# Four graph layers in one kernel: a base table for the sort, two accumulators for layer 0's sums, one last stage

## What is computed

```python
x = x + L0(h)   # attention: softmax over the edges of a source node, weighted rows summed at dst
x = x + L1(h)   # rows of dst, times a filter, summed at src; residual layers on the nodes
x = x + L2(h)   # a normed message per edge, summed at dst; gated update
x = x + L3(h)   # messages as below
# L3: agg = segment_sum(W * (h[dst] @ lin1.T), src);  return h + ssp(agg @ lin2.T + lin2_b)
# ssp(v) = softplus(v) - log(2)
# L0: out = segment_sum(msg, col);  out = where(deg > 0, out, xh)
```

## Time and profile before

| | |
|---|---|
| median of 3 runs | 7450.98 us |
| profiled execution | 7452.6 us, its span 7451.0 us |
| busy: TensorE / VectorE / GpSimd / ScalarE | 65% / 63% / 60% / 35% |
| sort: first to last send | 332.4 to 1584.9 us |
| layer 0's sums: first to last load issue of GpSimd | 2940.2 to 3433.1 us |
| last three stages | 7375.0 to 7451.0 us |

### The profile page before, as it was taken

The page is one execution under the profiler, slowest core; times in us unless marked ns, Lnnn a source line. Parts: engine busy times, 40 slices in busy tenths (PEclk is TensorE's granted clock), DMA queues, the critical chain, the costliest instruction groups (busy, mean ns, idle before and its releaser), DMA issues. The chain is left out here.

```text
span 7451.0 us, 136629 instructions
## 1 busy us (share of the span) xinstructions
PE 4824.4 (65%) x26170; PEld 3695.7 (50%) x26171; DVE 4677.1 (63%) x15439; ACT 2640.5 (35%) x6893; POOL 4448.7 (60%) x5261
## 2 busy tenths in 40 slices
PE   6777777730555554773566666666667664998896
PEld 4555555520444443662355555334555554666664
DVE  8666665634444443666555555777777775777776
ACT  2244444410222222664400000563333334444443
POOL 0165666652777777662277777207777771777774
PEclk9978787765555555666566667788888886778777
DMA  1144444460222222441133333103333321333332
GB/s 59 51 119 118 120 119 119 117 71 20 58 58 58 58 57 71 113 112 48 43 78 78 78 78 78 25 15 78 74 74 74 75 68 31 73 72 72 72 72 52
DMA packets 858580, 541.08 MB, mean 73 GB/s; under 512 B 652181, under 2 KB 757481, under 8 KB 858089
## 3 DMA queue, kind: packets, MB, share of 16 engines
q0 software_dynamic: 148032, 300.00, 14.9%
q1 hardware_dynamic: 608520, 192.51, 12.5%
q10 hardware_dynamic: 101920, 47.37, 2.6%
HBM read 411.68 MB, written 127.68 MB: 72 GB/s over the span
## 5 line engine op out<-in xcount | busy, mean ns | idle before, releaser
L1339 POOL DMA_INDIRECT l2e_rows<-l_rows,l2e_idx x832 | 847.2, 1018 | 566.9 <-DVE l2e_idx L1347 328.4
L798 POOL DMA_INDIRECT src_records<-sort_rec,sort_idx x784 | 768.5, 980 | 552.4 <-DVEq L676 319.4
L1339 POOL DMA_INDIRECT l1e_rows<-l_rows,l1e_idx x832 | 796.8, 958 | 490.0 <-DVE l1e_idx L1347 296.3
L1339 POOL DMA_INDIRECT l3e_rows<-l_rows,l3e_idx x832 | 804.1, 967 | 424.8 <-DVE l3e_idx L1347 221.4
L1222 POOL DMA_INDIRECT dst_rows<-l0d_out,l0d_idx x832 | 812.3, 976 | 276.5 <-issue 196.7
L2115 PE MATMUL l2e_pV<-l2e_rows,ident 128*128 128x512 f32 x416 | 302.3, 817 | 355.6 <-DMA l2e_rows<-l_rows,l2e_idx 355.1
L1194 PE MATMUL l0d_pX<-table,l0d_ohT 128*128 x1664 | 461.2, 457 | 86.3 <-issue 69.3
L1321 PE MATMUL l0m_pR<-l0m_rows,l0m_oh 128*128 128x129 f32 x1664 | 352.8, 378 | 200.2 <-DVE h_nodes L1292 140.9
L1685 PE MATMUL l1e_pG<-k_weights,l1e_dT 64*128 64x128 f32 x1664 | 220.5, 403 | 374.7 <-DVE l1e_prod L1714 371.7
L1194 PEld LDWEIGHTS l0d_pX<-table,l0d_ohT 128*128 128x128 f32 x1664 | 393.1, 326 | 139.8 <-issue 139.7
L1186 PE MATMUL l0d_pT<-identb,l0d_oh 128*128 128x128 bf16 x832 | 125.4, 305 | 472.8 <-DVE l0d_oh L1167 472.8
(11 more groups left out here) (406 smaller groups left out, 13955.7 us busy)
## 6 DMA issues: line engine op xcount, KB each, us to landing
sort_rows<-lo_rows SPq DMA_DIRECT2D x196, 256.0 KB
sort_rec<-rec ACTq DMA_DIRECT2D x98, 472.0 KB
l0m_rows<-dst_rows SPq DMA_DIRECT2D x416, 66.0 KB, 2.0
l0m_rows<-dst_rows POOLq DMA_DIRECT2D x416, 66.0 KB
l1e_rec<-src_records SPq DMA_DIRECT2D x832, 32.0 KB
l2e_lrow<-dst_local SPq DMA_DIRECT2D x208, 128.0 KB
l3e_rec<-src_records SPq DMA_DIRECT2D x832, 25.0 KB
l0d_meta<-src_records SPq DMA_DIRECT2D x832, 6.0 KB
```

The lines of the kernel that those rows point to most:

```text
L798: e.indirect_dma_start(kn.by_src_rec[:, :], bass.IndirectOffsetOnAxis(ap=r["idx"][:, st.quad, j:j + 1], axis=0), r["rec"][:, st.quad, j, : ...
L1339: e.indirect_dma_start(r["rows"][:, st.quad, j, 0:width], None, table[:, :], bass.IndirectOffsetOnAxis(ap=r["idx"][:, st.quad, j:j + 1], a ...
```

## The change

**The sort's base table.** The front's count of destinations keeps its tiles apart: step i's matmul multiplies with a matrix that has ones in column i only, so row i of `hd` gets the counts of step i. `offsets` makes from it, for each step (partition) and tile, the base of every block, as two numbers whose sum it is (`tile_base`, half and remainder, in 16 bits). In the sort, `drank` is then three matmuls: the one-hots of the step times "before", and row i of each part of the table, picked by one column of the identity (and of twice the identity) that is read 128 times. The copy `carry`, the row `dbase`, and the waits for them are gone.

**Record loads.** `load_records` moves from ScalarE to SyncE, one round later than the rows of keys; SyncE first waits for the clearing of the record buffers.

**Layer 0's sums.** Tiles 0 and 2 of a step add to `sums0`, tiles 1 and 3 to a second accumulator `odd`; an add waits for the last one of its own accumulator. `l0_table` clears `odd` too, and `l0_close` adds it to `sums0` with one instruction of 128 x 6321.

**The end of layer 3.** `l3_finish` replaces the three stages: per group of 7 blocks the product, clamp, exp, ln, the maximum, seven turns, and two additions; SyncE stores a group when its additions are done. PSUM holds two groups of products (four before), and nothing clears `AC`.

```diff
                                     row(kn, "b_att")[:, 0:2 * HEADS], ALU.add).then_inc(r["s_ok"], 1)
             e.wait_ge(r["pe"], n)
-            ch(e.tensor_reduce(kn.tot_dst[:, :], r["hd"][:, 0:GT * NB].rearrange("p (t b) -> p b t", b=NB), AX, ALU.add))
+            ch(e.tensor_copy(kn.tile_counts[:, :], r["hd"][:, 0:GT * NB]))
...
-                    e.matmul(r["hd"][:, 0:GT * NB], kn.onesh[:, :], r["hi"][:, i % 2, 0, :, :].rearrange("p t b -> p (t b)"),
+                    e.matmul(r["hd"][:, 0:GT * NB], r["to_row"][:, P - i:2 * P - i], r["hi"][:, i % 2, 0, :, :].rearrange("p t b -> p (t b)"),
...
+                     skip_group_check=True)
+            e.wait_ge(r["grouped"], 1)
+            e.matmul(r["small"][:, 2 * NB:3 * NB], kn.before[:, :], r["group"][:, :], start=True, stop=True,
+                     skip_group_check=True)
+            e.matmul(r["small"][:, 3 * NB:4 * NB], kn.ones[:, :], r["group"][:, :], start=True, stop=True,
                      skip_group_check=True).then_inc(r["sums"], 1)
...
+            counts = kn.tile_counts[:, :].rearrange("p (t b) -> p t b", b=NB)
+            e.tensor_reduce(r["group"][:, :], counts.rearrange("p t b -> p b t"), AX, ALU.add).then_inc(r["grouped"], 1)
...
+            ch(e.tensor_tensor(r["row"][:, 0, :], r["small"][:, 2 * NB:3 * NB], r["excl"][:, 0:NB], ALU.add))
+            for t in range(GT - 1):
+                ch.wait()
+                ch(e.tensor_tensor(r["row"][:, t + 1, :], r["row"][:, t, :], counts[:, t, :], ALU.add))
+            ch.wait()
+            rows = r["row"][:, :, :].rearrange("p t b -> p (t b)")
+            ch(e.tensor_scalar(kn.tile_base[:, 0, :], rows, 0.5, None, ALU.mult))
+            ch.wait()
+            ch(e.scalar_tensor_tensor(kn.tile_base[:, 1, :], kn.tile_base[:, 0, :], -2.0, rows, ALU.mult, ALU.add))
             e.wait_ge(r["counted"], 2)
...
+            def load_records(st):
+                wait_quad_free(e, r, "sent", st, GT)
+                e.dma_start(r["rec"][:, st.quad, :, 0:NREC], rec_tiles[:, bass.ds(st.i * GT, GT), :]
+                            ).then_inc(r[f"rec_ld{st.quad}"], 16)
+
             e.wait_ge(kn.low_st, 32)
-            run_steps(e, ch, [(load_rows, 0)], n)
+            e.wait_ge(r["cleared"], 1)
+            run_steps(e, ch, [(load_rows, 0), (load_records, 1)], n, 4)
...
-                e.wait_ge(r["carried"], st.i + 2)
...
-            run_steps(e, ch, [(load_records, 0), (wide_hot, 1), (low, 0), (keys, 2), (mask, 1), (carry, 2)], n, 4)
+            run_steps(e, ch, [(wide_hot, 1), (low, 0), (keys, 2), (mask, 1)], n, 4)
...
             def drank(st):
-                e.wait_ge(r["carried"], st.i + 1)
+                wait_step(e, r["hot"], st)
                 wait_step(e, r["dtaken"], st, 1)
-                e.matmul(r["drank"][:, 0:(GT + 1) * NB].rearrange("p (t b) -> p t b", b=NB), r["onerow"][0:1, :],
-                         r["dbase"][0:1, None, :].to_broadcast([1, GT + 1, NB]), start=True, stop=False,
-                         skip_group_check=True)
-                e.matmul(r["drank"][:, 0:GT * NB], kn.beforeh[:, :],
-                         r["ohhi"][:, st.quad, 0, :, :].rearrange("p t b -> p (t b)"), start=False, stop=False,
-                         skip_group_check=True)
-                for j in range(GT):
-                    ins = e.matmul(r["drank"][:, (j + 1) * NB:(GT + 1) * NB].rearrange("p (t b) -> p t b", b=NB),
-                                   kn.onesh[:, :], r["ohhi"][:, st.quad, 0, j:j + 1, :].to_broadcast([P, GT - j, NB]),
-                                   start=False, stop=(j == GT - 1), skip_group_check=True)
+                out = r["drank"][:, 0:GT * NB]
+                e.matmul(out, kn.beforeh[:, :], r["ohhi"][:, st.quad, 0, :, :].rearrange("p t b -> p (t b)"),
+                         start=True, stop=False, skip_group_check=True)
+                for k, t in enumerate((kn.twiceh, kn.identh)):
+                    ins = e.matmul(out, t[:, bass.ds(st.i, 1)].to_broadcast([P, P]), kn.tile_base[:, k, :],
+                                   start=False, stop=(k == 1), skip_group_check=True)
                 ins.then_inc(r["dranked"], 1)
...
             ch(e.memset(kn.sums0[:, :], 0.0))
+            ch(e.memset(kn.odd[:, :], 0.0))
             e.wait_ge(r["got"], 16 * NB)
...
-                wait_step(e, r["added"], st, 1)
                 for j in range(G):
-                    if j:
+                    if j == 1:
+                        wait_step(e, r["added"], st, 1)
+                    elif j:
+                        ch.until(at[j % 2])
+                    else:
                         ch.wait()
-                    acc = kn.sums0[:, bass.ds(blocks[j] * AW, AW)]
+                    acc = (kn.odd if j % 2 else kn.sums0)[:, bass.ds(blocks[j] * AW, AW)]
                     ins = e.tensor_tensor(acc, acc, sums(r, st, j), ALU.add)
                     if j < G - 1:
                         ch(ins)
+                        at[j % 2] = ch.done
...
             sums = kn.sums0[:, :].rearrange("p (b w) -> p b w", w=AW)
+            ch(e.tensor_tensor(kn.sums0[:, :], kn.sums0[:, :], kn.odd[:, :], ALU.add))
+            ch.wait()
...
+def l3_finish(kn):
+
+    whole = N // P
+
     def build(r):
+        def tensor(e, ch):
+            def product(k):
+                if k > 1:
+                    e.wait_ge(r["maxed"], k - 1)
+                src = wide(kn, kn.AC, k)
+                for h in range(2):
+                    ins = e.matmul(r["p"][:, k % 2, h, 0:SEC], mat(kn, "lin2"), src[:, h, :], start=True, stop=True)
+                ins.then_inc(r["product"], 1)
+
+            def turn(k):
+                e.wait_ge(r["maxed"], k + 1)
+                for q in halves(k):
+                    if q > 1:
+                        e.wait_ge(r["added"], q - 1)
+                    for j, b in enumerate(members(q)):
+                        ins = e.transpose(four(r["pA"], q)[:, j, :], kn.MT[:, b, :], kn.ident[:, :])
+                    ins.then_inc(r["turned"], 1)
+            product(0)
+            product(1)
+            for k in range(GROUPS):
+                if k + 2 < GROUPS:
+                    product(k + 2)
+                turn(k)
+
+        def vector(e, ch):
+            ch(e.tensor_scalar(r["less"][:, :], vec(kn, "lin2_b"), 1.0, -LN2, ALU.mult, ALU.add))
+
+            def clamp(k):
+                e.wait_ge(r["product"], k + 1)
+                if k > 1:
+                    e.wait_ge(r["maxed"], k - 1)
+                e.tensor_scalar(r["part"][:, k % 2, :, :], r["p"][:, k % 2, :, 0:SEC], vec(kn, "lin2_b"), CAP, ALU.add, ALU.min
+                                ).then_inc(r["clamped"], 1)
+
+            def keep(k):
+                x = group(kn.X, k)
+                e.tensor_tensor(x, x, group(kn.Hn, k), ALU.add).then_inc(r["kept"], 1)
+
+            def smooth(k):
+                e.wait_ge(r["logged"], k + 1)
+                e.scalar_tensor_tensor(wide(kn, kn.MT, k), r["p"][:, k % 2, :, 0:SEC], r["less"][:, 0:1],
+                                       r["part"][:, k % 2, :, :], ALU.add, ALU.max).then_inc(r["maxed"], 1)
+
+            def add(k):
+                e.wait_ge(r["kept"], k + 1)
+                for q in halves(k):
+                    e.wait_ge(r["turned"], q + 1)
+                    x = few_blocks(kn.X, q)
+                    e.tensor_tensor(x, x, four(r["pA"], q), ALU.add).then_inc(r["added"], 1)
+            clamp(0)
+            clamp(1)
+            ch.wait()
+            for k in range(GROUPS + 1):
+                if k < GROUPS:
+                    keep(k)
+                    smooth(k)
+                if k + 2 < GROUPS:
+                    clamp(k + 2)
+                if k:
+                    add(k - 1)
+
+        def scalar(e, ch):
+            e.preload_act_table_set("natural_log_exp_and_others")
+            for k in range(GROUPS + 1):
+                if k < GROUPS:
+                    e.wait_ge(r["clamped"], k + 1)
+                    ch(e.activation(r["part"][:, k % 2, :, :], r["part"][:, k % 2, :, :], ACT.Exp))
+                if k < GROUPS:
+                    ch.wait()
+                    e.activation(r["part"][:, k % 2, :, :], r["part"][:, k % 2, :, :], ACT.Ln, bias=kn.half1[:, 0:1], scale=0.5
+                                 ).then_inc(r["logged"], 1)
+
         def sync(e, ch):
-            full = (N // P) * P
-            e.dma_start(kn.out[0:full, :].rearrange("(b p) h -> p b h", p=P), kn.X[:, 0:N // P, :]).then_inc(r["st"], 16)
-            e.dma_start(kn.out[full:N, :], kn.X[0:N - full, N // P, :]).then_inc(r["st"], 16)
-            e.wait_ge(r["st"], 32)
-        return dict(sync=sync)
-    phase(kn, "store", build, sems=["st"])
+            out = kn.out[0:whole * P, :].rearrange("(b p) h -> p b h", p=P)
+            for k in range(GROUPS):
+                e.wait_ge(r["added"], 2 * k + 2)
+                last = min(GROUPS * (k + 1), whole)
```

(11 more changed lines are left out.)

66 lines of the change are left out of this document (18 added, 48 removed).

## The result

The changed kernel takes 7200.98 us (median of three runs, 7198.4 to 7212.5) against 7450.98: a ratio of 0.967, 95% interval 0.966 to 0.969. The profiled execution took 7198.4 us with a span of 7196.8, so the span fell by 254.2 us where 266.7 were forecast.

The account below looks back on a forecast made before the run. No engine bounds the whole; in the sort a ring of waits sets the pace. Sends -250.6, set-up +4, sums -3, merge +6.9, last stage -24 give -266.7: 7451.0 to 7184 us, range for 8 in 10 7163 to 7265.

Parts of the forecast that it names:

- the ring: Sort: waits linking GpSimd's sends, ScalarE's wait for them, its base-row copy and VectorE; 25.38 us for two steps.
- the new bound: Sort after the change: GpSimd's sends bound it at 10.22 us per step, -250.6 us; chance 0.66.
- The first rival: Sort: VectorE and TensorE, handing work to each other, hold a step at about 11 us, 7261 us; chance 0.20.
- the low clock: Sort: the clock falls to TensorE's low level, 13 us per step, 7458 us at worst; chance 0.03.
- the issue time alone: Sort: moving the loads and dropping the copy saves only their issue time, 7378 us; chance 0.05.
- the slower SyncE order: Sort: SyncE's queue delays key rows behind sends, closing in three steps; 7553 us at a 25 us load; chance 0.02.
- One sign: Sort: ScalarE's wait for landed sends would be gone and its idle time would lie with VectorE's compares.
- The ring is cut at both joints.: Sort: no wait for sends stands ahead of ScalarE's work, and VectorE needs no copy; part of the -250.6 us.
- the price per send, 1.278 us: Sort: GpSimd's time per send, issue gaps included, from the trace of before; 784 sends take 1001.9 us.
- the first row of the ledger: Sort: change of the sends' stretch, first to last; forecast -250.6 us, measured -228.8.
- `drank` on TensorE: Sort: three matmuls of the remaining shape cost at most 1.05 us per step, where `drank` took 2.21.
- Set-up: Before the sort: table operations about 1 us, SyncE's wait for clearing the records 3 us; +4 us, bounds 1 and 8.

Follow-up runs that it names:

- the second run: Kernel before with only the base table, record loads left on ScalarE: 8973.0 us (ratio 0.999); on another chip 7415.5 us (0.994).

## Why the prediction was right, and where it was off

The forecast was 7184 us with 7163 to 7265; measured 7201. Leaving the untouched stages aside, its terms came to -242.3 us instead of -266.7. The 11.9 us from those stages brought the measured time nearer to the forecast, and that is luck: without them it would be 7213.

**The ring and the new bound.** Right: the ring ran through ScalarE's wait for sends, and GpSimd's own sends are what is left. The first rival (11 us a step), the low clock, the issue time alone (57 us, where the loads alone gave 225) and the slower SyncE order did not come about; the granted clock in the sort rose from 0.80 to 0.88, and SyncE's order cost nothing: VectorE's 1.9 us per round at the key rows, seen in the waits, stand beside GpSimd's sends. One sign came out otherwise: ScalarE's idle time lies mostly before the landing of the record load (299.6 us) and less before VectorE's compares (121.6).

**"The ring is cut at both joints."** Half true. It rests on one cut: the loads alone give the 225 us, the table alone 42, and the table on top of the loads nothing in the sort (1019.8 against 1023.7 us). The forecast of the sum did not depend on it, but whoever had made only the table, on the argument that VectorE then needs no copy, would have been wrong by 170 us or more; I made that mistake in the expectation of the second run.

**The mis-sized term: the price per send, 1.278 us.** It measured 1.306, and 784 times 0.028 are the 22 us by which the first row of the ledger falls short. Some 17 of them are longer sends, 1.001 us instead of 0.980. I took the price from a trace in which GpSimd was idle for 5 us in every second step; there, fewer sends met VectorE's compares. With GpSimd busy all the time, each round's compares meet one: 0.045 us over the shortest send on average, 0.024 before. The other 5 us are a slip in the working: it spread the gaps named "issue", which stood before 695 of the 747 sends, over all 747, 0.298 us each, while the gap of the others was counted with GpSimd's waits; with GpSimd busy all the time it is 0.305 us before every send. The run with the compare twice shows the tie.

**`drank` on TensorE.** Two matmuls with the read-128-times column and one with ordinary weights take 63.1 us in 92 steps, 0.69 us a step (at most 1.05 forecast); the column costs nothing extra: 0.33 us for each of the three matmuls, 0.1 for each weight load.

**Set-up** +2.8 of 4. **Sums**: right that GpSimd's pattern binds and that shortening VectorE's part is worth nothing; -0.5 instead of -3. Wrong that the 80.5 us of VectorE's waits for itself would go: 70.1 are still there. **Merge** 6.75 us for 6.9, and 1.75 of that came back in the last additions of the stage, which went in two chains instead of one.

**The last stage**, 55.2 instead of 52 us: the form was right (stall, five times), its size too small: the working took a stall of about 2 us for all, and four of the five were 3.45, at the low clock (for which 8 us more were held ready in the bounds). Maxima end at 7.9, 13.0, 20.7, 28.4, 36.1 and 43.9 us after the first product; I had 8.5, 13.9, 20.6, 27.3, 34.1 and 40.8.

**The rest.** 11.9 us came from stages that the change doesn't touch. 5.4 of them lie between layer 1's node layers and layer 2's edges, 307.5 us here and 312.7 to 314.3 in the trace of before and in four later ones without TensorE's gaps, so it looks like scatter of this one execution. 4.1 are in layer 0's message stage, 1037 us before and 1029 to 1034 in five traces of kernels with a changed sort. Whether the sort leaves something behind that helps there, or the trace of before was the odd one, stays open.

## What to carry to other kernels

A wait at the head of a queue holds everything behind it, so look for every way on which that work reaches the engine that the wait is for, each engine's queue order included, and not only for the one that the list of waits names first; cutting one joint of a ring with two is worth little. When a stall goes, the freed engine's price per instruction is to be taken with all its neighbours awake: minimum plus what it meets, not the mean of a trace in which it rested. A second accumulator, a second buffer or a shorter chain pays only on the engine that binds the stage; relieve that one first, and then ask again.

## What I had not expected of the hardware

On two of the five chips of the experiments the kernel before takes 8999 and 9009 us instead of 7446 to 7458. Neither sends nor loads show it: with the loads alone, GpSimd's sends take 994 ns on average there, and a 66 KB load lands in 1.9 us. What differs is TensorE: gaps of 0.3 to 2.5 us between ready matmuls, named "issue". Two more things go with it: stalls on other engines that the profile names only "remote" (up to 20 us on ScalarE), and a lower granted clock, 0.67 to 0.68 over the whole execution of before against 0.72, and 0.72 against 0.81 in its sort (500 to 1300 us). On these two chips the kernels with a relieved sort show next to nothing (ratios of 0.995 to 1.004), while the last stage keeps its gain. Whether the gaps, the stalls and the clock have one cause, and which, stays open: no experiment here takes them apart.

The other surprise is the collision of VectorE's compares with GpSimd's sends: up to 0.8 us for one send that starts 0.04 us after a compare.
